# GpSimd in place of VectorE for the argument of the prefix exponent and the low part of block 0's mixed tiles

## The chip, the cores and the metric

One core of a Trainium2 chip runs the whole program. The metric is the device time of one execution in microseconds (us); the kernel before has a median of 1816.48 us over three runs (1815.62 to 1816.57).

## What is computed

The input x has 4 sequences of 1024 positions with 1024 channels; fside has the same shape. First a gated linear recurrence in both directions along the positions (for each channel), then a feed-forward layer with a quantised gelu, then the residual:

```
ek  = exp(min(fside, 30));  ekv = ek * fside
nf, df = forward scans  a = a * decay + ekv,  b = b * decay + ek
nb, db = the same scans backward
num = nf + nb - ekv + exp(min(u + fside, 30)) * fside      (den likewise, without the last factor)
mix = sigmoid(x) * num / max(den, 1e-8) * (0.8 + 0.2 tf)    (decay and tf per sequence, from cond)
h   = mix @ W1.T            (W1: 4096 x 1024)
a   = gelu(round(h / 0.1) * 0.1)
out = x + a @ W2.T          (W2: 1024 x 4096)
```

## The kernel before, in words

A sequence is cut in two halves of 512 positions; a half of a sequence is a block, so there are 8 blocks, and each has 8 tiles (128 channels x 512 positions). Tile g belongs to block g // 8. Even blocks are the late halves (`late` in `tile_of`), odd ones the early halves; blocks run late half first. A late tile needs the state that the early half leaves for it. It is had without a scan: the kernel loads the early half's fside tile as VP, makes the argument EKP = RAMP * ln(decay) + min(VP, 30), takes the exponent on ScalarE with its sum (the prefix of den), and multiplies with VP (L926, the prefix of num). `prefix_argument(g)` makes this argument with two VectorE instructions, L915 (TENSOR_SCALAR) and L918 (SCALAR_TENSOR_TENSOR). EKP is one buffer; VP, V, R, EK, EKV, BON, NUM, DEN have two (index g % 2).

A tile's work on VectorE is split in four parts. Part 0, `weigh`: L926, L929, L931. Part 1, `forward`: scans L959 and L961, and the first step of the reciprocal of the tile before (L937). Part 2, `backward`: scans L978 and L983, with L940 and the output m_st of the tile before (L947) between them, and then `prefix_argument(g + 1)`. Part 3, `sums`: L992 to L1012; its last instruction raises s_gate, on which the loads of V and R of tile g + 2 wait. ScalarE runs the exponents of tile g + 1 (`exps`, which first wait for s_arg of a late tile), then the reciprocal of tile g, then its tanh.

The mixed tile goes to TensorE as a high and a low 16-bit float. For block 0, ScalarE makes the high part (`mix_hi`, L681), and VectorE subtracts it from m_st for the low part (`mix_lo`, L1037), behind part 3 of the next tile. TensorE multiplies each tile of block 0 as it comes (`first_hidden`, L483), then the rest of block 0's hidden layer (L496), and then, block after block, the output product (L562) and the hidden layer of the next block by seven products of halves (L506). While TensorE works on block n, VectorE and ScalarE make the tiles of block n + 1, five of them beside the hidden layer and three beside the output, in an order that is written out by hand in `hidden_block` and behind it.

GpSimd only issues transfers: in a loop over s = 0..7 it waits until R of tile s has landed, and then issues the cast of one eighth of W1 to 16 bits in DRAM (L449), with a cast of W2 at every odd s (L451); then four more casts of W2 (L454) as TensorE's hidden layer proceeds, and 24 copies (L459) during block 0's output. SyncE issues all loads and stores in one hand-written order; in block 0 the first ring loads of weights, which wait for the first two casts, stand ahead of the loads of tiles 2 and 3.

Of the kernel before, what the change touches and what calls it, by code (L numbers as in the profile page):

```python
# [6 lines left out]
ALU = mybir.AluOpType  # L7
# [8 lines left out]
CLIP = 30.0  # L16
# [17 lines left out]
def adaln_ffn_kernel(nc, x, fside, cond, w, u, w1, w2, out):  # L34
    B, HALVES, CT, _, T = x.shape
# [5 lines left out]
    BLOCKS = B * HALVES  # L41
# [11 lines left out]
    with ExitStack() as ctx:  # L53
# [3 lines left out]
        def sem(name):  # L57
            return ctx.enter_context(nc.semaphore(name))
# [21 lines left out]
        mix0 = mo_flat[:, 0:CT * 2 * T].rearrange("p (c a t) -> p c a t", c=CT, a=2)  # L80
# [3 lines left out]
        m_st = sb("m_st", [P, 3, 2, T], F32)  # L84
# [10 lines left out]
        VP = sb("VP", [P, 2, T], F32)  # L95
        EK = sb("EK", [P, 2, T + 1], F32)
        EKV = sb("EKV", [P, 2, T + 1], F32)
        BON = sb("BON", [P, 2, T], F32)
        NUM = sb("NUM", [P, 2, T], F32)
        DEN = sb("DEN", [P, 2, T], F32)  # L100
        EKP = sb("EKP", [P, T], F32)
        RCP = sb("RCP", [P, T], F32)
        RAMP = sb("RAMP", [P, T], F32)
# [22 lines left out]
        lndec = sb("lndec", [P, B, CT], F32)  # L126
# [7 lines left out]
        flag = sb("flag", [1, 1], I32)  # L134
# [11 lines left out]
        s_lndec = sem("s_lndec")  # L146
        s_ramp = sem("s_ramp")
# [7 lines left out]
        s_vp = [sem(f"s_vp{k}") for k in range(2)]  # L155
        s_argr = sem("s_argr")
        s_arg = sem("s_arg")
        s_ekp = sem("s_ekp")
        s_dot = sem("s_dot")
        s_ekx = sem("s_ekx")  # L160
# [17 lines left out]
        s_gate = sem("s_gate")  # L178
# [4 lines left out]
        s_mixhi = sem("s_mixhi")  # L183
        s_mix = sem("s_mix")
# [33 lines left out]
        s_flag = sem("s_flag")  # L218
# [5 lines left out]
        def tile_of(g):  # L224

            n, t = g // CT, g % CT
            return n % BLOCKS // 2, n % 2 == 0, (t % 2) * KH + t // 2, CT * (n // 2) + t
# [9 lines left out]
        def m_slot(g):  # L237
            return (g // 2) % 3
# [205 lines left out]

        @block.gpsimd
        def _(pool):
            for s in range(STEPS):
                pool.wait_ge(s_r[s % 2], 16 * (s // 2 + 1))
                pool.dma_start(w1_half[s], w1_full[s]).then_inc(s_w1cast[s], 16)  # L449
                if s % 2 == 1:  # L450
                    pool.dma_start(w2_half[s // 2], w2_full[s // 2]).then_inc(s_w2cast[s // 2], 16)  # L451
            for d in range(DT // 2, DT):
                pool.wait_ge(s_h0, FPS * (d - 1))
                pool.dma_start(w2_half[d], w2_full[d]).then_inc(s_w2cast[d], 16)  # L454
            for s in range(STEPS):
                pool.wait_ge(s_y, 2 + s)
                pool.wait_ge(s_w1cast[s], 16)
                for r, h, k in ((WP1, 0, 0), (WP2, 0, 1), (WP4, 1, 1)):
                    pool.dma_start(w1s[s][:, r, :, :], w1_quads[s][:, h, :, k, :]).then_inc(s_w1copy[s], 16)  # L459
            for d in range(DT):  # L460
                pool.wait_ge(s_w2cast[d], 16)
            for s in range(STEPS):
                pool.wait_ge(s_w1copy[s], 16 * 3)

        @block.tensor
        def _(pe):
# [409 lines left out]
        def _(dve):  # L876
            v = nc.vector
# [30 lines left out]
                dve.wait_ge(s_lndec, B + 1)  # L908
                dve.wait_ge(s_setup, 6 + B)

            def prefix_argument(g):
                b, late, c, pg = tile_of(g)
                if late:
                    dve.wait_ge(s_ramp, 3)
                    v.tensor_scalar(EKP[:, :], RAMP[:, :], lndec[:, b, c:c + 1], None, ALU.mult).then_inc(s_argr, 1)  # L915
                    dve.wait_ge(s_vp[pg % 2], 16 * (pg // 2 + 1))
                    dve.wait_ge(s_argr, pg + 1)
                    v.scalar_tensor_tensor(out=EKP[:, :], in0=VP[:, pg % 2, :], scalar=CLIP, in1=EKP[:, :],  # L918
                                           op0=ALU.min, op1=ALU.add).then_inc(s_arg, 1)

            def weigh(g):
                b, late, c, pg = tile_of(g)
                k = g % 2
# [91 lines left out]
            def part(p, g):  # L1015

                last = g - 1 if g % CT else None
                if p == 0:
                    weigh(g)
                if p == 1:  # L1020
                    forward(g, last)
                if p == 2:
                    backward(g, last)
                    if g % CT < CT - 1:
                        prefix_argument(g + 1)
                if p == 3:
                    sums(g)

            def divide(g):
                newton(g, 0)  # L1030
                newton(g, 1)
                mixed_out(g)

            def mix_lo(g):
                c = tile_of(g)[2]
                dve.wait_ge(s_mixhi, g + 1)
                v.tensor_tensor(mix0[:, c, 1, :], m_st[:, m_slot(g), g % 2, :], mix0[:, c, 0, :],  # L1037
                                ALU.subtract).then_inc(s_mix, 1)

            def operand_sums(n, q):  # L1040
                g, at = CT * n + 2 * q, KH * (n - 1) + q
# [78 lines left out]
                                       op0=ALU.mult, op1=ALU.not_equal, accum_out=bad[:, at:at + 1]).then_inc(s_chk, 1)  # L1120

            factors()
            prefix_argument(0)
            for t in range(CT):
                for p in range(4):
                    part(p, t)
                    if p == 3 and t > 0:
                        mix_lo(t - 1)
            divide(CT - 1)
            mix_lo(CT - 1)  # L1130

            def hidden_block0(g0):
                for s in range(STEPS):
# [17 lines left out]
            def hidden_block(n, nxt, g0):  # L1151
                for s in range(STEPS):
                    if nxt:
                        if s == 0:
                            prefix_argument(g0)
                        elif s % 2 == 0:
                            part(3, g0 + s // 2 - 1)
                        else:
                            part(1, g0 + s // 2)
                    if s >= 2:  # L1160
                        act_lo(n, s - 2, 1)
                    if s >= 1:
                        quantise22(n, s - 1)
                    if nxt:
                        part(0 if s % 2 == 0 else 2, g0 + s // 2)
                    seed_u4(n, s)
                    if s >= 1:
                        act_lo(n, s - 1, 0)
                if nxt:
                    part(3, g0 + 3)  # L1170
                act_lo(n, LAST - 1, 1)
                if nxt:
                    part(0, g0 + 4)
                quantise22(n, LAST)
                if nxt:
                    part(1, g0 + 4)
                act_lo(n, LAST, 0)
                if nxt:
                    part(2, g0 + 4)
                act_lo(n, LAST, 1)  # L1180
# [71 lines left out]
            def general_block(m):  # L1252
                n = BLOCKS + m
                for t in range(CT):
                    g = CT * n + t
                    prefix_argument(g)
                    weigh(g)
                    forward(g, None)
                    backward(g, None)
                    sums(g)  # L1260
                    newton(g, 0)
                    newton(g, 1)
                    if m > 0:
                        dve.wait_ge(g_h, FT * m)
                    scaled_out(g, ogain_gneg, mix_gen[:, tile_of(g)[2], :])
                for d in range(DT):
                    result(n, d, g_y, DT * m + d + 1, 1.0)
# [46 lines left out]
```

## Time and profile before

| | before |
|---|---|
| median of 3 runs | 1816.48 us |
| the profiled execution's own time | 1813.9 us |
| its span, first to last instruction | 1811.6 us |
| TensorE busy | 1699.9 us, 94% |
| VectorE busy | 1279.5 us, 71% |
| ScalarE busy | 1043.5 us, 58% |
| GpSimd busy | 24.6 us, 1% |

The times of instructions come from the one profiled execution. Start times are counted from the first instruction. A row of the timeline gives start, duration, engine, line, operation and tiles; in square brackets stands how long the engine was idle before it and what ended that. An engine's consecutive instructions overlap a little, so that the distance of two starts, not the duration, is what an instruction costs in a stream. TensorE's busy time is modelled.

### The profile page before, as it was taken

To read this page: it belongs to the slowest core of one execution; us is meant where nothing else is said; L and a number is where in the kernel's file an instruction comes from. 1 tells how busy PE (TensorE), PEld (TensorE's weight loads), DVE (VectorE), ACT (ScalarE), POOL (GpSimd) and SP (SyncE) were. 2 spreads that over 40 slices of the span, in tenths; PEclk is the share of its full clock that TensorE was granted. 3 is DMA by queue.
4 is the path that set the end of the run, shared out by engine and by line. 5 is a ranking of instruction groups with operands and counts; after the bars stand their busy time and mean duration, and the time that the engine had idled before them with its cause. 6 is when DMAs were issued, how large, how long until landed. Compare 5 with 4: busy or idle time off the path is not lost. (4 is left out here: it accounts for less than half of the span.)

```text
span 1811.6 us, 27451 instructions
## 1 busy us (share of the span) xinstructions
PE 1699.9 (94%) x10882; PEld 1067.0 (59%) x10882; DVE 1279.5 (71%) x2008; ACT 1043.5 (58%) x1422; POOL 24.6 (1%) x44
## 2 busy tenths in 40 slices
PE   1459999999999999999999999999999999999998
PEld 0124434687448854588447864488545874478643
DVE  8988885878866786779866777678966687633211
ACT  5458843687437863498526874388634885255300
POOL 0000021000000000000000000000000000000000
PEclk9679999999999999999999999999999999999999
DMA  8747785665546644655446545466445654365442
GB/s 239 178 128 204 253 286 198 204 198 181 162 147 204 195 139 155 198 191 202 162 133 203 187 158 174 144 217 204 156 144 192 195 180 152 120 194 158 145 129 82
DMA packets 109238, 321.16 MB, mean 177 GB/s; under 512 B 12720, under 2 KB 12720, under 8 KB 108592
## 3 DMA queue, kind: packets, MB, share of 16 engines
q1 hardware_dynamic: 106416, 296.28, 50.1%
q0 software_dynamic: 2688, 23.07, 5.5%
q8 instruction: 87, 1.43, 0.3%
q14 instruction: 47, 0.39, 0.1%
HBM read 310.91 MB, written 48.23 MB: 198 GB/s over the span
## 5 line engine op out<-in xcount | busy, mean ns | idle before, releaser
L562 PE MATMUL ps<-act,w_ring 128*128 128x512 f16 x4096 | 890.7, 380 | 4.4 <-DVE y_out L1111 4.4
L506 PE MATMUL ps<-mo,w_ring 128*128 128x256 f16 x6272 | 690.6, 273 | 11.0 <-ACT ps L706 6.1
L562 PEld LDWEIGHTS ps<-act,w_ring 128*128 128x128 f16 x4096 | 401.4, 98 | 485.7 <-issue 8.8
L506 PEld LDWEIGHTS ps<-mo,w_ring 128*128 128x128 f16 x6272 | 612.5, 98 | 90.1 <-issue 7.8
L1102 DVE SCALAR_TENSOR_TENSOR act<-a,act 128x1024 f16<-128x1024 f32 x128 | 156.2, 1221 | 134.7 <-ACT act L755 134.7
L1111 DVE SCALAR_TENSOR_TENSOR y_out<-ps,x_in 128x512 f32<-128x512 f32 x64 | 44.1, 690 | 175.1 <-PE ps L562 107.3
L763 ACT ACTIVATE q<-chk_full 128x1024 int8<-128x1024 f32 x64 | 67.0, 1047 | 144.5 <-DMA chk_full<-in_w_dram 144.5
L749 ACT ACTIVATE a<-q 128x1024 f32<-128x1024 int16 x128 | 135.3, 1057 | 14.6 <-DVE act L1102 10.3
L755 ACT ACTIVATE act<-a 128x1024 f16<-128x1024 f32 x128 | 134.2, 1049 | 0.9
L483 PE MATMUL ps<-mo,w_ring 128*128 128x512 f16 x128 | 42.6, 509 | 89.3 <-DVE mo L1037 89.3
L1119 DVE SCALAR_TENSOR_TENSOR chk_full<-q,chk_full 128x1024 f32<-128x1024 int8 x64 | 78.1, 1220 | 43.8 <-ACT q L763 43.8
L696 ACT ACTIVATE mo<-a 128x1024 f16<-128x1024 f32 x28 | 29.6, 1057 | 128.8 <-DVE a L1048 128.8
L650 ACT ACTIVATE EK<-V 128x512 f32<-128x512 f32 x64 | 39.9, 623 | 109.6 <-DMA V<-in_fside_dram 109.3
L646 ACT ACTIVATE EKP<-EKP 128x512 f32<-128x512 f32 x32 | 20.2, 631 | 133.7 <-DVE EKP L918 133.5
L1085 DVE SCALAR_TENSOR_TENSOR ps<-sp,ps 128x512 f32<-128x512 f32 x56 | 38.8, 692 | 73.7 <-PE ps L506 66.9
L483 PEld LDWEIGHTS ps<-mo,w_ring 128*128 128x128 f16 x128 | 15.4, 125 | 116.0 <-issue 55.8
L496 PE MATMUL ps<-mo,w_ring 128*128 128x512 f16 x384 | 83.0, 379 | 0.0
L670 ACT ACT_TABLE_LOAD x64 | 82.1, 1283 | 1.1
L643 ACT ACT_TABLE_LOAD x64 | 82.1, 1283 | 1.1
L733 ACT ACTIVATE q<-ps 128x512 int16<-128x512 f32 x56 | 33.3, 594 | 85.6 <-PE ps L506 85.6
L978 DVE TENSOR_TENSOR_SCAN EK<-EK,decay 128x512 f32<-128x512 f32 x64 | 81.7, 1277 | 0.1
L983 DVE TENSOR_TENSOR_SCAN EKV<-EKV,decay 128x512 f32<-128x512 f32 x64 | 81.6, 1276 | 0.0
(94 smaller groups left out, 1461.1 us busy)
## 6 DMA issues: line engine op xcount, KB each, us to landing
w_ring<-w1s SPq DMA_DIRECT2D x168, 512.0 KB, 3.7
w_ring<-w_half SPq DMA_DIRECT2D x144, 512.0 KB, 4.2
chk_full<-in_w_dram SPq DMA_DIRECT2D x64, 512.0 KB, 4.6
V<-in_fside_dram SPq DMA_DIRECT2D x64, 256.0 KB, 4.7
R<-in_x_dram SPq DMA_DIRECT2D x64, 256.0 KB, 4.8
w_half<-in_w_dram POOLq DMA_DIRECT2D x16, 1024.0 KB, 7.9
x_in<-in_x_dram SPq DMA_DIRECT2D x64, 256.0 KB, 5.3
out_dram<-y_out SPq DMA_DIRECT2D x64, 256.0 KB, 4.8
```

The lines of the kernel that those rows point to most:

```text
L496: mm = pe.matmul(bank[4 * (s % 2) + j][:, :], w1_ring[:, k, f, c, :], mix0[:, c, p, :], start=(c == 0 and p == 0), stop=(c == CT - 1 and p ...
L506: mm = pe.matmul(dst[:, f, :], wp_ring[:, k, r, f, q, :], mo[:, op, q, p, :], start=(fresh and f == 0 and q == 0 and p == 0), stop=(q == K ...
L562: mm = pe.matmul(y_ps[y][:, :], w2_ring[:, k, f, :], act[:, a, p, :], start=(a == 0 and p == 0), stop=(a == FT - 1 and p == 1))
L643: sc.preload_act_table_set(EXP_SET)
L670: sc.activation(R[:, g % 2, :], R[:, g % 2, :], ACT.Tanh, scale=0.5).then_inc(s_tanh, 1)
L749: sc.activation(a32[:, 2 * h:2 * h + 2, :], q16[:, s % 2, 2 * h:2 * h + 2, :], ACT.Gelu_apprx_tanh, scale=QSTEP).then_inc(s_gelu, 1)
L755: sc.activation(act[:, f:f + 2, 0, :], a32[:, 2 * h:2 * h + 2, :], ACT.Copy, scale=ACT_SCALE).then_inc(s_ahi, 1)
L763: sc.activation(chk_i8, chk_full[:, :], ACT.Copy, scale=W_SCALE).then_inc(s_chki8, 1)
L978: v.tensor_tensor_scan(EK[:, k, 0:T][:, ::-1], EK[:, k, 0:T][:, ::-1], dec(b, c), EK[:, k, T:T + 1], ALU.add, ALU.mult).then_inc(s_dbwd, 1)
L983: v.tensor_tensor_scan(EKV[:, k, 0:T][:, ::-1], EKV[:, k, 0:T][:, ::-1], dec(b, c), EKV[:, k, T:T + 1], ALU.add, ALU.mult).then_inc(s_nbwd, 1)
L1102: v.scalar_tensor_tensor(out=act[:, f:f + 2, 1, :], in0=a32[:, 2 * h:2 * h + 2, :], scalar=ACT_SCALE, in1=act[:, f:f + 2, 0, :], op0=ALU.m ...
L1119: v.scalar_tensor_tensor(out=chk_full[:, :], in0=chk_i8, scalar=1.0 / W_SCALE, in1=chk_full[:, :], op0=ALU.mult, op1=ALU.not_equal, accum_ ...
```

## The change

`prefix_argument` moves from VectorE's program to GpSimd's. There it has three instructions in place of two, since the clip and the sum are made apart: RAMP * ln(decay) into EKP, min(VP, 30) into BON[g % 2] (free until ScalarE writes it for the same tile; the new wait on s_gate guards it), and their sum into EKP. A new semaphore s_kp stands between the last two, and a wait on s_dot guards EKP before it is written again. `mix_lo` moves too, unchanged. In GpSimd's order the argument of tile 0 stands ahead of the first cast; then, for each s, the cast of W1, the argument of tile s + 1, the cast of W2 if there is one, and the low part of tile s - 1. The arguments of blocks 2, 4 and 6 follow behind the last copies. The general path, which only runs when a check on the inputs fails, gets its arguments from GpSimd as well. In `hidden_block` the order of the parts stays.

```diff
--- before.py
+++ after.py
@@ -155,6 +155,7 @@
         s_vp = [sem(f"s_vp{k}") for k in range(2)]
         s_argr = sem("s_argr")
         s_arg = sem("s_arg")
+        s_kp = sem("s_kp")
         s_ekp = sem("s_ekp")
         s_dot = sem("s_dot")
         s_ekx = sem("s_ekx")
@@ -444,11 +445,41 @@
 
         @block.gpsimd
         def _(pool):
+            pl = nc.gpsimd
+
+            def prefix_argument(g):
+                b, late, c, pg = tile_of(g)
+                if late:
+                    pool.wait_ge(s_ramp, 3)
+                    pool.wait_ge(s_lndec, B + 1)
+                    if pg > 0:
+                        pool.wait_ge(s_dot, pg)
+                    pl.tensor_scalar(EKP[:, :], RAMP[:, :], lndec[:, b, c:c + 1], None, ALU.mult).then_inc(s_argr, 1)
+                    pool.wait_ge(s_vp[pg % 2], 16 * (pg // 2 + 1))
+                    pool.wait_ge(s_argr, pg + 1)
+                    if g >= 2:
+                        pool.wait_ge(s_gate, g - 1)
+                    pl.tensor_scalar(BON[:, g % 2, :], VP[:, pg % 2, :], CLIP, None, ALU.min).then_inc(s_kp, 1)
+                    pool.wait_ge(s_kp, pg + 1)
+                    pl.tensor_tensor(EKP[:, :], BON[:, g % 2, :], EKP[:, :], ALU.add).then_inc(s_arg, 1)
+
+            def mix_lo(g):
+                c = tile_of(g)[2]
+                pool.wait_ge(s_mixhi, g + 1)
+                pl.tensor_tensor(mix0[:, c, 1, :], m_st[:, m_slot(g), g % 2, :], mix0[:, c, 0, :],
+                                ALU.subtract).then_inc(s_mix, 1)
+
+            prefix_argument(0)
             for s in range(STEPS):
                 pool.wait_ge(s_r[s % 2], 16 * (s // 2 + 1))
                 pool.dma_start(w1_half[s], w1_full[s]).then_inc(s_w1cast[s], 16)
+                if s + 1 < CT:
+                    prefix_argument(s + 1)
                 if s % 2 == 1:
                     pool.dma_start(w2_half[s // 2], w2_full[s // 2]).then_inc(s_w2cast[s // 2], 16)
+                if s > 0:
+                    mix_lo(s - 1)
+            mix_lo(CT - 1)
             for d in range(DT // 2, DT):
                 pool.wait_ge(s_h0, FPS * (d - 1))
                 pool.dma_start(w2_half[d], w2_full[d]).then_inc(s_w2cast[d], 16)
@@ -457,10 +488,18 @@
                 pool.wait_ge(s_w1cast[s], 16)
                 for r, h, k in ((WP1, 0, 0), (WP2, 0, 1), (WP4, 1, 1)):
                     pool.dma_start(w1s[s][:, r, :, :], w1_quads[s][:, h, :, k, :]).then_inc(s_w1copy[s], 16)
+            for g in range(2 * CT, CT * BLOCKS):
+                prefix_argument(g)
             for d in range(DT):
                 pool.wait_ge(s_w2cast[d], 16)
             for s in range(STEPS):
                 pool.wait_ge(s_w1copy[s], 16 * 3)
+
+            pool.wait_ge(s_flag, 1)
+            needs_general = pool.value_load(flag[0:1, 0:1], min_val=0, max_val=1)
+            with pool.If(needs_general > 0):
+                for g in range(CT * BLOCKS, 2 * CT * BLOCKS):
+                    prefix_argument(g)
 
         @block.tensor
         def _(pe):
@@ -907,16 +946,6 @@
                 v.tensor_scalar(lndec[:, :, :], lndec[:, :, :], LN_DECAY_MIN, None, ALU.max).then_inc(s_lndec, 1)
                 dve.wait_ge(s_lndec, B + 1)
                 dve.wait_ge(s_setup, 6 + B)
-
-            def prefix_argument(g):
-                b, late, c, pg = tile_of(g)
-                if late:
-                    dve.wait_ge(s_ramp, 3)
-                    v.tensor_scalar(EKP[:, :], RAMP[:, :], lndec[:, b, c:c + 1], None, ALU.mult).then_inc(s_argr, 1)
-                    dve.wait_ge(s_vp[pg % 2], 16 * (pg // 2 + 1))
-                    dve.wait_ge(s_argr, pg + 1)
-                    v.scalar_tensor_tensor(out=EKP[:, :], in0=VP[:, pg % 2, :], scalar=CLIP, in1=EKP[:, :],
-                                           op0=ALU.min, op1=ALU.add).then_inc(s_arg, 1)
 
             def weigh(g):
                 b, late, c, pg = tile_of(g)
@@ -1021,8 +1050,6 @@
                     forward(g, last)
                 if p == 2:
                     backward(g, last)
-                    if g % CT < CT - 1:
-                        prefix_argument(g + 1)
                 if p == 3:
                     sums(g)
 
@@ -1030,12 +1057,6 @@
                 newton(g, 0)
                 newton(g, 1)
                 mixed_out(g)
-
-            def mix_lo(g):
-                c = tile_of(g)[2]
-                dve.wait_ge(s_mixhi, g + 1)
-                v.tensor_tensor(mix0[:, c, 1, :], m_st[:, m_slot(g), g % 2, :], mix0[:, c, 0, :],
-                                ALU.subtract).then_inc(s_mix, 1)
 
             def operand_sums(n, q):
                 g, at = CT * n + 2 * q, KH * (n - 1) + q
@@ -1120,14 +1141,10 @@
                                        op0=ALU.mult, op1=ALU.not_equal, accum_out=bad[:, at:at + 1]).then_inc(s_chk, 1)
 
             factors()
-            prefix_argument(0)
             for t in range(CT):
                 for p in range(4):
                     part(p, t)
-                    if p == 3 and t > 0:
-                        mix_lo(t - 1)
             divide(CT - 1)
-            mix_lo(CT - 1)
 
             def hidden_block0(g0):
                 for s in range(STEPS):
@@ -1151,12 +1168,10 @@
             def hidden_block(n, nxt, g0):
                 for s in range(STEPS):
                     if nxt:
-                        if s == 0:
-                            prefix_argument(g0)
-                        elif s % 2 == 0:
+                        if s % 2 == 1:
+                            part(1, g0 + s // 2)
+                        elif s > 0:
                             part(3, g0 + s // 2 - 1)
-                        else:
-                            part(1, g0 + s // 2)
                     if s >= 2:
                         act_lo(n, s - 2, 1)
                     if s >= 1:
@@ -1253,7 +1268,6 @@
                 n = BLOCKS + m
                 for t in range(CT):
                     g = CT * n + t
-                    prefix_argument(g)
                     weigh(g)
                     forward(g, None)
                     backward(g, None)
```

## Rows read from the trace of the kernel before

**Rows 1.** The page: busy time and share of each engine; the slices.
```profile
PE 1699.9 (94%) x10882; PEld 1067.0 (59%) x10882; DVE 1279.5 (71%) x2008; ACT 1043.5 (58%) x1422; POOL 24.6 (1%) x44
...
PE   1459999999999999999999999999999999999998
...
DVE  8988885878866786779866777678966687633211
ACT  5458843687437863498526874388634885255300
```

**Rows 2.** Timeline of PE: the start of its unbroken work, and its later gaps.
```profile
123.34 8.59 PE L483 MATMUL ps<-mo,w_ring 128*128 128x512 f16 x32 [8.33 <-DVE mo L1037]
131.76 83.04 PE L496 MATMUL ps<-mo,w_ring 128*128 128x512 f16 x384
...
546.10 3.28 PE L506 MATMUL ps<-mo,w_ring 128*128 128x256 f16 x26 [0.86 <-DVE mo L1054]
550.53 9.66 PE L506 MATMUL ps<-mo,w_ring 128*128 128x256 f16 x87 [1.15 <-ACT ps L706]
...
759.34 5.84 PE L506 MATMUL ps<-mo,w_ring 128*128 128x256 f16 x52 [0.32 <-ACT ps L706]
```

**Rows 3.** Timeline of DVE in block 0: the first argument, one tile's period, the last tile.
```profile
8.85 0.49 DVE L915 TENSOR_SCALAR EKP<-RAMP,lndec 128x512 f32<-128x512 f32 x1
...
60.52 0.48 DVE L915 TENSOR_SCALAR EKP<-RAMP,lndec 128x512 f32<-128x512 f32 x1
...
61.72 0.69 DVE L992 TENSOR_TENSOR DEN<-DEN,EK 128x512 f32<-128x512 f32 x1
...
65.91 0.68 DVE L1037 TENSOR_TENSOR mo<-m_st,mo 128x512 f16<-128x512 f32 x1
66.51 0.68 DVE L926 SCALAR_TENSOR_TENSOR EKV<-EKP,VP 128x512 f32<-128x512 f32 x1
...
74.99 0.48 DVE L915 TENSOR_SCALAR EKP<-RAMP,lndec 128x512 f32<-128x512 f32 x1
...
123.87 0.69 DVE L937 TENSOR_TENSOR DEN<-DEN,RCP 128x512 f32<-128x512 f32 x1 [0.59 <-ACT RCP L666]
```

**Rows 4.** Groups by line and shape, whole span: busy us, mean ns of one.
```profile
L992 DVE TENSOR_TENSOR DEN<-DEN,EK 128x512 f32<-128x512 f32 x64 | 43.8, 684 | 0.0
L959 DVE TENSOR_TENSOR_SCAN NUM<-decay,pre_n,EKV 128x512 f32<-128x512 f32 x32 | 41.0, 1280 | 0.8
L929 DVE TENSOR_SCALAR EK<-EK 128x512 f32<-128x512 f32 x64 | 27.0, 422 | 2.0 <-ACT EK L650 1.8
...
L650 ACT ACTIVATE EK<-V 128x512 f32<-128x512 f32 x64 | 39.9, 623 | 109.6 <-DMA V<-in_fside_dram 109.3
```

**Rows 5.** The page's DMA issues: count, KB each, median us to landing.
```profile
R<-in_x_dram SPq DMA_DIRECT2D x64, 256.0 KB, 4.8
w_half<-in_w_dram POOLq DMA_DIRECT2D x16, 1024.0 KB, 7.9
```

**Rows 6.** Timeline of ACT at the start: the first exponent of an argument.
```profile
10.18 0.63 ACT L646 ACTIVATE EKP<-EKP 128x512 f32<-128x512 f32 x1 [0.94 <-DVE EKP L918]
```

**Rows 7.** Timelines of POOL and DVE: a cast's issue and the scan beside it.
```profile
30.08 0.49 POOL L449 DMA_DIRECT2D w_half<-in_w_dram  x1 [19.44 <-DMA R<-in_x_dram]
...
29.75 1.28 DVE L983 TENSOR_TENSOR_SCAN EKV<-EKV,decay 128x512 f32<-128x512 f32 x1
```

**Rows 8.** Timelines of DVE and ACT at the output of block 1.
```profile
507.31 0.69 DVE L918 SCALAR_TENSOR_TENSOR EKP<-VP,EKP 128x512 f32<-128x512 f32 x1 [7.43 <-DMA VP<-in_fside_dram]
...
508.03 0.63 ACT L646 ACTIVATE EKP<-EKP 128x512 f32<-128x512 f32 x1 [17.58 <-DVE EKP L918]
...
511.38 0.63 ACT L664 ACTIVATE RCP<-DEN 128x512 f32<-128x512 f32 x1 [0.87 <-DVE DEN L1003]
```

**Rows 9.** Stretches of 4 us: busy (count) of each engine, PE clock, DMA.
```profile
120.00:124.00 4.00, 0.66 (x2) 0.29 (x3) 3.38 (x9) 3.00 (x4) 0.00 (x0) 0.50 0.09 16
...
128.00:132.00 4.00, 4.00 (x21) 1.78 (x19) 0.00 (x0) 3.03 (x4) 0.00 (x0) 1.00 0.00 0
```

## The prediction

> **What bounds the kernel now.** I read the busy shares and the slices first. TensorE is busy 94% of the span, but its row of slices begins 1, 4, 5 and is full from the fourth slice on, while VectorE is full over those first slices [rows 1]. So there are two stretches with different limits. TensorE's own row of time gives the border: from 131.76 us it works almost without a gap to the end, and what it loses is little: about 2 us (0.86 and 1.15) where it enters a block with late tiles in preparation, against 0.32 us where the tiles in preparation are early ones [rows 2]. Behind the border VectorE's share is spare time; ahead of it the time is whatever makes the last mixed tile. Everything that moves that border moves the end one for one.
>
> Ahead of the border VectorE is back to back: a late tile takes 14.47 us (60.52 to 74.99, the start of the same instruction in two tiles), with no idle time in it; its first wait of the stretch worth naming is 0.59 us for ScalarE's reciprocal of the last tile [rows 3]. ScalarE waits for VectorE there, and TensorE sits idle 8.33 us before its last two tiles [rows 2]. VectorE sets the border.
>
> **The change, part by part.** (1) Two instructions per late tile leave VectorE: L915 and L918 hold it from 60.52 to 61.72, so 1.20 us. Seven of these lie in block 0's back-to-back stretch (tiles 1 to 7): 8.4 us. (2) mix_lo leaves it: 65.91 to 66.51, 0.60 us. Six of the eight are in the stream (tiles 0 to 5), 3.6 us; that of tile 6 lies in the 0.59 us wait for the reciprocal and is worth nothing, and that of tile 7 is the last step of the path [rows 3]. Together 12.0 us off VectorE's stream, 12.7 us a tile in place of 14.47. What comes next on that path is then ScalarE and the transfers. ScalarE's slices there are about half full, some 7 us in a tile [rows 1], and it would get the argument early in the tile. A load of R lands 4.8 us after its issue [rows 5], and is issued a whole tile ahead of its use. Both fit in 12.7 us. The casts go out behind the argument and the mixed tile of the step before, so later within a tile, and the first behind the first argument. The ring loads that wait for the first two casts stand in SyncE's queue ahead of the loads of tiles 2 and 3; those wait for VectorE's gate, the end of the sums of tiles 0 and 1, anyhow, and a cast lands 7.9 us after its issue [rows 5], so I cost this at nothing. The cover fails if that landing grows to well over 12 us.
>
> (3) GpSimd gets four instructions for these tiles in place of three: ramp times a scalar, min, add, and the subtraction. No row shows GpSimd at 128x512. Bounds: not less than VectorE's own 0.48 and 0.68, since nothing suggests that it is the faster engine; not more than the slowest 128x512 row, the scan with 1.28 [rows 3, 4]. I take 0.62 for the two with one tensor input, ScalarE's row for 128x512, and 1.25 for the two with two inputs, near the scan: together 3.74 us a tile (bounds 2.3 and 5.1). The Trainium skill (GPSIMD Engine Reference, section Elementwise — side-by-side cycle accounting) gives 4497 ns for a two-input add of 2048 elements; an estimate from it is about 1.2 us for 512, and the sum by it would be the same within 1 us.
>
> (4) At both ends GpSimd's length is bare. The first argument takes VectorE from 8.85 to ScalarE's start at 10.18, 1.33 us [rows 3, 6]; on GpSimd 0.62 + 0.62 + 1.25 and some 0.24 us of handing over, 2.73: +1.4 us (bounds +0.3 and +2.8). The last mix_lo: 1.25 for 0.69, +0.6 us (0 to +0.6).
>
> (5) Whether GpSimd's time is beside VectorE's or in its place decides the sign. What the rows show: a two-input instruction of 512 elements takes 0.684 us on VectorE, a one-input one 0.422 [rows 4]. So VectorE reads two operands' worth at once, and one-input work uses that for double speed: it has two ways into the memory and nearly each of its instructions in this stretch keeps both in use. GpSimd reads the same partitions. The only case of both together is a cast's issue at 30.08 under a scan that keeps its usual 1.28 us [rows 7], which writes a few descriptors and reads no tensor, so it excludes nothing. My forecast takes it that one of the two stands still while the other reads. The page SBUF — State Buffer of the Trainium skill, section Who interferes with whom, speaks against this change in the same sense: a VectorE instruction with two SBUF inputs and a GpSimd instruction that reads SBUF exclude each other for a whole instruction. No row here can confirm it.
>
> Then each GpSimd instruction takes its length from VectorE's stream, less the 0.09 us by which VectorE's instructions overlap anyhow (0.69 long, 0.60 apart) [rows 3]. Arguments: 7 x (2.49 - 0.27 - 1.20) = +7.1 us. Mixed tiles: 7 x (1.25 - 0.09) - 3.6 = +4.5 us (seven now, since tile 6's falls beside the sums). With both ends, +13.6 us at the border.
>
> (6) Beyond the border, 24 more arguments leave VectorE, 28.8 us, all under TensorE. At the entry to a late-fed block the path runs through one of them: VP of the last tile arrives at 507.31, VectorE adds, ScalarE starts at 508.03 and has 0.87 us to spare before its next wait ends [rows 8]. On GpSimd min and add take 1.87 us where 0.69 stood, so ScalarE starts about 1.2 us later, of which 0.87 us is covered: +0.3 us at each of three such entries, +1 us (bounds 0 and +4.5, if each instruction must also wait for one of VectorE's). That VectorE no longer stands 7.43 us for VP gives nothing, as its next result waits for that same ScalarE chain.
>
> Sum: 13.6 + 1 = +14.6 us on the profiled execution's 1813.9 us (span 1811.6), 1828.5. The median of the runs stands 2.6 us above that execution, so 1831 us. By bounds: with GpSimd at VectorE's durations 7 x (1.65 - 0.27 - 1.20) + 7 x 0.59 - 3.6 + 0.3 = +2.1 us, 1819; with 1.28 for each instruction 7 x (3.84 - 0.27 - 1.20) + 7 x 1.19 - 3.6 + 3.4 + 4.5 = +29 us, 1846. I hold durations near the middle likelier than either end.
>
> **Rivals.** *Side by side (faster).* If the two engines read without disturbing each other, the terms are -12.0 + 1.4 + 0.6 + 1 = -9.0 us: 1807.5 us (1804 to 1811). For it: 12.0 us of plain VectorE work on the path that sets the border, a GpSimd that is 1% busy [rows 1], and the cast that disturbed no scan. Against: the two ways into memory that VectorE's rows show in use. It decides from the point at which a GpSimd instruction costs VectorE less than four tenths of its length (12.0 - 2.0 us left to lose, against 7 x 3.74 = 26 us of GpSimd time). TensorE's last tile could add up to 3 us in it, if the earlier tile 6 leaves a pause in which the clock falls: it stands at 0.50 before that burst and at 1.00 after 128 us [rows 9]; I expect the pause too short.
>
> *Partly in each other's way.* Scans take about twice a plain instruction's time for as many elements (1.28 against 0.684) [rows 4], and may leave half the reads free; the argument falls mostly beside scans. Then some 3 us of the 12.0 are left or lost after the ends: 1813 to 1820, centre 1817.
>
> *The work is moved but arrives late.* GpSimd's queue now has, ahead of an argument, the wait for R, a cast (0.49 us) and the mixed tile of two tiles before, which waits for ScalarE's copy. An argument may start 0.7 us into a tile (behind L926) and its exponent is needed at the tile's end: 12.7 - 0.7 - 2.5 - 0.7, some 8 us, are spare. Were GpSimd held out by VectorE's stream until VectorE itself has to wait for the argument, a tile would cost 12.7 + 2.5 + 0.7 (the exponent) and more: about 17 us, +20 us in all, 1838. This is within the slower side.
>
> **How the numbers follow.** Forecast (one stands still for the other) 0.47; held out until VectorE waits 0.08; partly 0.15; side by side 0.30. "The same" is within 0.2%, 3.6 us, about what a measurement of this kernel can tell from no change: most of "partly" and the lowest part of the forecast, 0.16; slower 0.54; faster 0.30. The forecast's own range is 1819 to 1843. The range that should hold 8 in 10 must reach into the faster case: 1805 to 1840.
>
> **What would show it.** In the changed kernel's profile: the distance between the starts of L926 in two of block 0's tiles, 12.7 us if side by side, about 16 by my forecast; VectorE's two-input instructions longer than 0.69 us, or idle time between them, where a GpSimd instruction runs; GpSimd's own mean at L915's and L918's successors, 0.62 and 1.25; TensorE's border at 145 us, or at 122; the first exponent at 11.6; and TensorE's gaps at entries to late-fed blocks of 2 us still. I am wrong if VectorE's instructions keep their 0.68 us beside GpSimd's.

## The result, and the profile after

The changed kernel takes 1832.73 us (median of 4 runs, 1831.88 to 1834.77) where the kernel before took 1816.05 us on the same chip: a ratio of 1.0095, 95% interval 1.0077 to 1.0112, so 0.95% slower. The forecast was 1831 us, its own range 1819 to 1843.

First the page of the changed kernel, its busy shares and GpSimd's slices, then GpSimd's groups by shape (busy us, mean ns of one, idle time before and what ended it). The lines of the file have shifted: GpSimd's L457, L462 and L464 are the product, the clip and the sum, L469 is the low part; VectorE's L955 was L926, and TensorE's L522, L535, L545 and L601 were L483, L496, L506 and L562.

```profile
PE 1706.5 (93%) x10882; PEld 1067.3 (58%) x10882; DVE 1289.6 (70%) x1936; ACT 1045.7 (57%) x1422; POOL 201.2 (11%) x148
...
POOL 4530021121110000111120000012120000000000
```
```profile
L462 POOL TENSOR_SCALAR BON<-VP 128x512 f32<-128x512 f32 x32 | 65.3, 2039 | 664.4 <-DMA VP<-in_fside_dram 663.0 <-POOL EKP L457 0.3
L457 POOL TENSOR_SCALAR EKP<-RAMP,lndec 128x512 f32<-128x512 f32 x32 | 50.5, 1578 | 314.0 <-DVE EKV L955 306.2 <-DVE lndec L946 7.8
L464 POOL TENSOR_TENSOR EKP<-BON,EKP 128x512 f32<-128x512 f32 x32 | 43.0, 1344 | 2.7
L469 POOL TENSOR_TENSOR mo<-m_st,mo 128x512 f16<-128x512 f32 x8 | 17.3, 2168 | 44.3 <-ACT mo L720 44.3
```

VectorE has 72 instructions fewer (64 of the arguments, 8 low parts) and is yet busy some 10 us longer than before [rows 1]: some of those that stayed became longer.

TensorE's timeline, the start of its unbroken work and later gaps:

```profile
130.56 9.98 PE L522 MATMUL ps<-mo,w_ring 128*128 128x512 f16 x32 [7.05 <-POOL mo L469]
140.37 83.04 PE L535 MATMUL ps<-mo,w_ring 128*128 128x512 f16 x384
...
558.20 3.28 PE L545 MATMUL ps<-mo,w_ring 128*128 128x256 f16 x26 [1.98 <-DVE mo L1075]
562.56 89.24 PE L545 MATMUL ps<-mo,w_ring 128*128 128x256 f16 x816 [1.09 <-ACT ps L745]
...
1258.38 24.61 PE L545 MATMUL ps<-mo,w_ring 128*128 128x256 f16 x224 [0.43 <-DVE q L1116]
```

The border is at 140.37 where it was at 131.76 [rows 2]: 8.6 us of the 18.5 us by which the span grew. At the entry to block 2 the same matmuls stand at 562.56 against 550.53, 12.0 us later; at the end it is 18.2 us. So about half of the loss lies behind the border.

Here is why VectorE's stream became longer. One tile of block 0, VectorE first, then GpSimd, in the changed kernel:

```profile
41.42 0.69 DVE L955 SCALAR_TENSOR_TENSOR EKV<-EKP,VP 128x512 f32<-128x512 f32 x1
...
42.49 1.06 DVE L960 TENSOR_TENSOR EKV<-EK,V 128x512 f32<-128x512 f32 x1
43.66 1.28 DVE L988 TENSOR_TENSOR_SCAN NUM<-decay,pre_n,EKV 128x512 f32<-128x512 f32 x1
44.86 1.56 DVE L990 TENSOR_TENSOR_SCAN DEN<-decay,pre_d,EK 128x512 f32<-128x512 f32 x1
46.36 1.75 DVE L966 TENSOR_TENSOR DEN<-DEN,RCP 128x512 f32<-128x512 f32 x1
...
54.52 1.51 DVE L1038 TENSOR_TENSOR NUM<-NUM,V 128x512 f32<-128x512 f32 x1
...
56.68 0.69 DVE L955 SCALAR_TENSOR_TENSOR EKV<-EKP,VP 128x512 f32<-128x512 f32 x1
```
```profile
42.33 1.57 POOL L457 TENSOR_SCALAR EKP<-RAMP,lndec 128x512 f32<-128x512 f32 x1 [1.61 <-DVE EKV L955]
44.04 2.18 POOL L462 TENSOR_SCALAR BON<-VP 128x512 f32<-128x512 f32 x1
46.31 1.26 POOL L464 TENSOR_TENSOR EKP<-BON,EKP 128x512 f32<-128x512 f32 x1
53.09 2.40 POOL L469 TENSOR_TENSOR mo<-m_st,mo 128x512 f16<-128x512 f32 x1 [5.52 <-ACT mo L720]
```

The instructions that became L960, L990, L966 and L1038, in the kernel before:

```profile
53.11 0.69 DVE L931 TENSOR_TENSOR EKV<-EK,V 128x512 f32<-128x512 f32 x1
...
55.11 1.26 DVE L961 TENSOR_TENSOR_SCAN DEN<-decay,pre_d,EK 128x512 f32<-128x512 f32 x1
56.30 0.69 DVE L937 TENSOR_TENSOR DEN<-DEN,RCP 128x512 f32<-128x512 f32 x1
...
64.58 0.68 DVE L1009 TENSOR_TENSOR NUM<-NUM,V 128x512 f32<-128x512 f32 x1
```

Four of VectorE's instructions are longer than their usual selves, each beside one of GpSimd's four: L960 by 0.37 us (1.06 for 0.69), L990 by 0.30, L966 by 1.06, L1038 by 0.83. Together 2.56 us. The tile takes 56.68 - 41.42 = 15.26 us, and 14.47 - 1.20 - 0.60 + 2.56 is 15.23. Nothing else changed in it. GpSimd waits too: L462 takes 2.18 us where it starts under a scan that already runs and 1.49 at the kernel's start, where VectorE is idle; L469 takes 2.40 us under the row of two-input sums and 1.15 at the end of block 0, where VectorE is idle.

### The profile page after: what moved, and what is told of

Read it like the earlier page. It is cut to its first block and busy times, and to the rows that moved or that the text cites. A ratio compares the mean times of both kernels' runs of the same rounds, so it can differ in the third digit from the quotient of the medians.

```text
span 1830.1 us, 27520 instructions
## 1 busy us (share of the span) xinstructions
PE 1706.5 (93%) x10882; PEld 1067.3 (58%) x10882; DVE 1289.6 (70%) x1936; ACT 1045.7 (57%) x1422; POOL 201.2 (11%) x148
## 5 line engine op out<-in xcount | busy, mean ns | idle before, releaser
L601 PE MATMUL ps<-act,w_ring 128*128 128x512 f16 x4096 | 889.5, 379 | 4.9 <-DVE y_out L1132 4.9
L545 PE MATMUL ps<-mo,w_ring 128*128 128x256 f16 x6272 | 694.0, 273 | 17.5 <-DVE mo L1075 9.0
L601 PEld LDWEIGHTS ps<-act,w_ring 128*128 128x128 f16 x4096 | 401.1, 98 | 485.2 <-issue 7.6
L545 PEld LDWEIGHTS ps<-mo,w_ring 128*128 128x128 f16 x6272 | 612.2, 98 | 100.8 <-issue 13.4
L1123 DVE SCALAR_TENSOR_TENSOR act<-a,act 128x1024 f16<-128x1024 f32 x128 | 156.9, 1226 | 136.2 <-ACT act L794 136.2
L462 POOL TENSOR_SCALAR BON<-VP 128x512 f32<-128x512 f32 x32 | 65.3, 2039 | 664.4 <-DMA VP<-in_fside_dram 663.0
L522 PE MATMUL ps<-mo,w_ring 128*128 128x512 f16 x128 | 46.5, 546 | 94.0 <-POOL mo L469 94.0
L522 PEld LDWEIGHTS ps<-mo,w_ring 128*128 128x128 f16 x128 | 16.4, 133 | 123.7 <-issue 63.8
L457 POOL TENSOR_SCALAR EKP<-RAMP,lndec 128x512 f32<-128x512 f32 x32 | 50.5, 1578 | 314.0 <-DVE EKV L955 306.2
L535 PE MATMUL ps<-mo,w_ring 128*128 128x512 f16 x384 | 83.0, 379 | 0.0
```

The costliest lines, as they stand in the source:

```text
L462: pl.tensor_scalar(BON[:, g % 2, :], VP[:, pg % 2, :], CLIP, None, ALU.min).then_inc(s_kp, 1)
L522: mm = pe.matmul(bank[4 * s + j][:, :], w1_ring[:, slots[2 * s + j // 2], j % 2, c, :], mix0[:, c, p, :], start=(t == 0 and p == 0), stop= ...
L535: mm = pe.matmul(bank[4 * (s % 2) + j][:, :], w1_ring[:, k, f, c, :], mix0[:, c, p, :], start=(c == 0 and p == 0), stop=(c == CT - 1 and p ...
L545: mm = pe.matmul(dst[:, f, :], wp_ring[:, k, r, f, q, :], mo[:, op, q, p, :], start=(fresh and f == 0 and q == 0 and p == 0), stop=(q == K ...
L601: mm = pe.matmul(y_ps[y][:, :], w2_ring[:, k, f, :], act[:, a, p, :], start=(a == 0 and p == 0), stop=(a == FT - 1 and p == 1))
L1123: v.scalar_tensor_tensor(out=act[:, f:f + 2, 1, :], in0=a32[:, 2 * h:2 * h + 2, :], scalar=ACT_SCALE, in1=act[:, f:f + 2, 0, :], op0=ALU.m ...
```

## The experiments

Each is compared with the kernel before on its own chip (ratio, 95% interval); borders are TensorE's first L496 in the profiled execution, 131.76 us before. A difference in us behind a ratio is that ratio times the time of the kernel before. The diffs show only the lines that matter. In the profiled executions of these runs ln(decay) is ready 0.2 to 0.8 us sooner than in the one of the kernel before (8.01 to 8.65 us in place of 8.82), a difference that no edit before it explains, and it lies in the borders. What block 0's stream itself gained or lost is therefore read from the first to the last of its eight L926, 98.99 us before. Where nothing else is said, the whole computation is done.

**One part alone: the low parts.**

```diff
-                    if p == 3 and t > 0:
-                        mix_lo(t - 1)        # VectorE, block 0
+                if s > 0:
+                    mix_lo(s - 1)            # GpSimd, behind the casts of step s
...
             def mixed_out(g):
+                if 6 <= g < CT + 6:
+                    dve.wait_ge(s_mix, g - 5)
```

The last wait is not in the changed kernel; it keeps a mixed tile from being overwritten before its low part is made.

> Only the eight low parts of block 0's mixed tiles are on GpSimd; all arguments stay on VectorE. Theory (the two engines exclude each other while they read): in the changed kernel each low part lengthened VectorE's L1038 from 0.68 to 1.51 us, so 7 x 0.83 = +5.8 us, less 6 x 0.60 = 3.6 us that leave VectorE, and +0.5 us for the bare last one: +2.7 us on before, and L1038's successor at 1.5 us in block 0. Rival (side by side): -3.6 + 0.5 = -3.1 us, with VectorE's instructions at 0.68 us.

Measured: 1814.18 us, ratio 0.9995 (0.9985 to 1.0004), which is -0.9 us; border 132.17, +0.4 us. Neither number came out (+2.7 and -3.1 us were expected); the lengthened instructions did. GpSimd's queue had no arguments in it, so the low parts ran at other places than in the changed kernel, four of the six in the stream beside L1025 and two beside a scan (L972):

```profile
35.86 1.53 DVE L1025 SCALAR_TENSOR_TENSOR NUM<-R,NUM 128x512 f32<-128x512 f32 x1
...
67.73 1.99 DVE L972 TENSOR_TENSOR_SCAN NUM<-decay,pre_n,EKV 128x512 f32<-128x512 f32 x1
...
67.01 1.62 POOL L452 TENSOR_TENSOR mo<-m_st,mo 128x512 f16<-128x512 f32 x1 [14.51 <-ACT mo L692]
```

The scan takes 1.99 us in place of 1.28, +0.71 us, and L1025 1.53 in place of 0.69, +0.84 us, where 0.60 leave. The stream is 100.12 us long, 1.1 us more than before, and 4 x 0.84 + 2 x 0.71 - 3.6 = +1.2. So a low part moved was worth nothing at either of the two places where it fell.

**One part alone: block 0's arguments.**

```diff
-            prefix_argument(0)               # VectorE
-                    if g % CT < CT - 1:
+                    if g % CT < CT - 1 and g >= CT:
                         prefix_argument(g + 1)
+            prefix_argument(0)               # GpSimd, three instructions
+                if s + 1 < CT:
+                    prefix_argument(s + 1)
```

> Only block 0's arguments are on GpSimd; later arguments and all low parts stay on VectorE. Theory: a tile's three GpSimd instructions cost VectorE 0.37 + 0.30 + 1.06 = 1.73 us (L960, L990, L966 of the changed kernel) where 1.20 us leave, 7 x 0.53 = +3.7 us, and the first argument comes 3.2 us later (4.5 us of GpSimd for 1.3): +6.9 us on before, TensorE's unbroken stretch at about 138.7. Rival (side by side): -8.4 + 3.2 = -5.2 us.

Measured: 1821.38 us, ratio 1.0034 (1.0021 to 1.0047), which is +6.2 us; border 139.22, +7.5 us.

```profile
139.22 83.04 PE L518 MATMUL ps<-mo,w_ring 128*128 128x512 f16 x384
```

The theory had +6.9 us: the time is 0.7 us below it and the border 0.6 above. The stream is 102.68 us long, +3.7 us as computed, and the first L926 starts at 13.98 in place of 10.93. This part carries 7.5 of the 8.6 us by which the border moved in the changed kernel.

**One part alone: the arguments of blocks 2, 4 and 6.** GpSimd's loop stands behind the copies, and VectorE keeps only tiles 0 to 7.

```diff
+            for g in range(2 * CT, CT * BLOCKS):
+                prefix_argument(g)           # GpSimd, three instructions
...
-                    if g % CT < CT - 1:
+                    if g < CT - 1:
                         prefix_argument(g + 1)
...
-                            prefix_argument(g0)
+                            pass
```

> Only the arguments of blocks 2, 4 and 6 are on GpSimd; block 0 is as before. In the changed kernel TensorE lost 9.7 us more behind its border than before, some 2 us of it at each of three block entries. Theory (a longer chain from VP to the exponent, 3.4 us of GpSimd for 0.7): all of that stays, +9 us, with the border at 131.8 unmoved. Rival (those losses follow from the disturbed block 0, or from the low parts): under +1 us.

Measured: 1824.59 us, ratio 1.0051 (1.0035 to 1.0068), +9.3 us; border 131.63, unmoved. The loss behind the border (9.6 us in the changed kernel) comes from these 24 arguments, with block 0 undisturbed. Its size is less certain than that: TensorE's way from the border to its last work is 1674.35 us in the profiled execution of the kernel before and 0.8 to 2.8 us longer in those of six runs here that change nothing behind the border, so some 1 to 3 us of the 9.6, and of the 12.2 in this run's own profile, may be that one execution. The three parts by themselves add up to -0.9 + 6.2 + 9.3 = +14.6 us where the whole cost 17.2; with some 2 to 3 us of uncertainty on each, the difference is not more than noise.

**Half of each argument: only the product on GpSimd.**

```diff
+                    pl.tensor_scalar(EKP[:, :], RAMP[:, :], lndec[:, b, c:c + 1], None, ALU.mult).then_inc(s_argr, 1)   # GpSimd
-                    v.tensor_scalar(EKP[:, :], RAMP[:, :], lndec[:, b, c:c + 1], None, ALU.mult).then_inc(s_argr, 1)    # VectorE
```

> GpSimd makes only the product RAMP * ln(decay) of every argument, with one tensor input; the clip and sum stay on VectorE as one instruction, and so do the low parts. Theory of exclusion with the price by instruction: VectorE loses 0.37 us a tile and is rid of 0.60, 7 x -0.23 = -1.6 us, and +1.1 us at the start: -0.5 us in block 0. Behind the border, theory of the long chain: nothing lost, since the product is made before VP arrives: in all -0.5 us, the same as before. Rival (later losses come from disturbing VectorE): several us slower still.

Measured: 1814.78 us, ratio 0.9997 (0.9988 to 1.0007); border 131.41. The forecast of -0.5 us came out in both. In block 0 the price by instruction holds: the stream is 97.42 us long, 1.6 us less than before (0.37 paid for 0.60, seven times), and the first L926 starts 1.1 us later. Behind the border nothing is lost beyond what the unchanged runs show, although GpSimd makes 24 products there beside VectorE's work: what hurts there is what comes behind VP's landing, the clip and the sum.

**The disturbance by itself.** Three runs keep all the work of before and add 16 GpSimd instructions of 128x512 in block 0, two behind each L926. Their results are used by nobody.

```diff
+                for j in range(2):
+                    pl.tensor_tensor(a32[:, 2 + j, :], RAMP[:, :], RAMP[:, :], ALU.add)        # first run
+                    pl.memset(a32[:, 2 + j, :], 1.0)                                           # second
+                    pl.tensor_scalar(a32[:, 2 + j, :], RAMP[:, :], 2.0, None, ALU.mult)        # third
```

The diff leaves out the waits: each of the 16 starts when the one before it has ended, and ScalarE waits for the last of them before its work on block 0's hidden layer.

> The kernel before, unchanged in all its work, with 16 added GpSimd instructions of two 128x512 float32 inputs in block 0, two behind each L926, whose results nobody uses. It measures the disturbance by itself. Theory: VectorE stands still while GpSimd reads, about 1.0 us each: +16 us, TensorE's unbroken stretch at about 148, VectorE's two-input instructions of 1.6 to 2.1 us in weigh, forward and backward. Rival (side by side; the changed kernel lost by order and by GpSimd's lateness): within 0.5 us of before.

> As the run with 16 added two-input instructions, but they are 16 fills (MEMSET) of the same size, which write and read nothing. Theory (it is the reading that excludes): within 1 us of before. Rival (any GpSimd access to the memory holds VectorE): about +0.5 us each, +8 us.

(A fill writes its tile and reads none; that is what the sentence above means.)

> As the run with 16 added two-input instructions, but with one input each (TENSOR_SCALAR). Theory: 0.3 to 0.4 us each, as L960 and L990 showed in the changed kernel, though each lasts 1.5 us: +5 to +6 us. Rival (VectorE is held for the whole length of a GpSimd instruction): 16 x 1.5 = +24 us.

Measured: two inputs 1825.09 us, ratio 1.0059 (1.0043 to 1.0074), border 141.48, +9.7 us; fills 1815.96 us, ratio 1.0004 (0.9994 to 1.0013), border 131.73; one input 1818.85 us, ratio 1.0026 (1.0016 to 1.0035), border 135.93, +4.2 us. The timelines of VectorE and GpSimd with two inputs:

```profile
56.25 1.41 DVE L944 TENSOR_TENSOR EKV<-EK,V 128x512 f32<-128x512 f32 x1
57.76 1.87 DVE L972 TENSOR_TENSOR_SCAN NUM<-decay,pre_n,EKV 128x512 f32<-128x512 f32 x1
...
56.01 1.09 POOL L456 TENSOR_TENSOR a<-RAMP 128x512 f32<-128x512 f32 x1 [12.26 <-issue]
57.19 1.37 POOL L456 TENSOR_TENSOR a<-RAMP 128x512 f32<-128x512 f32 x1
```

with one input:

```profile
69.22 0.98 DVE L944 TENSOR_TENSOR EKV<-EK,V 128x512 f32<-128x512 f32 x1
...
71.50 1.56 DVE L974 TENSOR_TENSOR_SCAN DEN<-decay,pre_d,EK 128x512 f32<-128x512 f32 x1
...
69.01 1.52 POOL L456 TENSOR_SCALAR a<-RAMP 128x512 f32<-128x512 f32 x1 [10.15 <-issue]
70.61 2.25 POOL L456 TENSOR_SCALAR a<-RAMP 128x512 f32<-128x512 f32 x1
```

and with fills:

```profile
66.78 0.69 DVE L944 TENSOR_TENSOR EKV<-EK,V 128x512 f32<-128x512 f32 x1
67.58 1.28 DVE L972 TENSOR_TENSOR_SCAN NUM<-decay,pre_n,EKV 128x512 f32<-128x512 f32 x1
...
66.52 1.27 POOL L456 MEMSET a<- 128x512 f32 x2 [7.22 <-issue]
```

So side by side falls: two-input instructions of 1.09 and 1.37 us took 0.72 and 0.59 us from VectorE, one-input instructions of 1.52 and 2.25 us only 0.29 and 0.30, and two fills of 0.6 us nothing. The rows even give the moment of release. VectorE's L944 should have ended at 56.94 and ended at 57.66, so it got going at 56.97, 0.96 us after GpSimd's start and 0.1 us before GpSimd's end; in the changed kernel L966 got going 0.15 us before L464 ended. Two inputs thus held VectorE for very nearly the whole instruction. With one input it is otherwise: L944 got going 0.5 us after the start of an instruction that lasts 1.52, and L974, like L960 and L990 in the changed kernel, 1.0 to 1.1 us before the end of GpSimd's. That VectorE waits just for the part in which GpSimd reads fits all of these rows, and the fills, but no row shows GpSimd's reading by itself. This is the step where the rule of the Trainium skill (SBUF — State Buffer, section Who interferes with whom) and the runs meet: reading against two inputs excludes, writing does not, as it says; that the pair is held "for the whole instruction" the rows with two inputs come close to and those with one do not bear out. I had expected 1.0 us each for the first run. The stream is 108.12 us long there, +9.1 us for 14 of the 16, so 0.65 us each: GpSimd's instruction starts 0.24 us ahead of L944 and 0.57 us ahead of L972, and that much of the hold costs VectorE nothing, where in the changed kernel L464 starts 0.05 us ahead of L966 and costs 1.06. One input cost 0.3 us each in the same count, at the low end of what I had expected.

**A late signal without any reading.** In blocks 2, 4 and 6, VectorE makes the arguments as before, but ScalarE also waits for 12 small fills that GpSimd makes behind VP's landing.

```diff
+                    for j in range(12):
+                        if fills > 0:
+                            pool.wait_ge(s_kp, fills)
+                        nc.gpsimd.memset(unused[:, :], 1.0).then_inc(s_kp, 1)
+                        fills += 1
                     act_e.wait_ge(s_arg, pg + 1)
+                    act_e.wait_ge(s_kp, 12 * (pg - CT + 1))
```

> The kernel before, with every argument made by VectorE as ever, but in blocks 2, 4 and 6 ScalarE's exponent also waits for 12 small fills (MEMSET 128x128) that GpSimd makes one after the other once VP has landed. GpSimd reads nothing, so VectorE is not disturbed; only the exponent is late, by some 2 to 4 us behind VP's landing as in the run with only the late blocks' arguments on GpSimd. Theory (those lose 9 us by a longer chain from VP to the exponent): +6 to +12 us, with TensorE's idle time of 3 us in place of 2 at the entries to blocks 2, 4 and 6 and small gaps in the hidden layers of blocks 1, 3 and 5. Rival (they lose it because GpSimd's reading holds VectorE): within 1 us of before.

Measured: 1820.74 us, ratio 1.0033 (1.0021 to 1.0045), +6.0 us. ScalarE's exponent at the output of block 1, and TensorE's entry to block 2:

```profile
510.39 0.63 ACT L661 ACTIVATE EKP<-EKP 128x512 f32<-128x512 f32 x1 [18.75 <-POOL unused L471]
...
547.84 93.76 PE L519 MATMUL ps<-mo,w_ring 128*128 128x256 f16 x842 [1.98 <-DVE mo L1069]
```

The exponent is 2.4 us later than before (508.03 [rows 8]), and TensorE enters block 2 at 547.84 for 546.10 [rows 2]. Lateness alone gives 6.0 of the 9.3 us, about two thirds, though the intervals of the two runs overlap; it falls at the entries (1.7 to 2.2 us each). The small gaps in hidden layers, which I had expected here too, did not come: none waits for VectorE's L1095 (L1116 in the changed kernel). They are the work of the exclusion, and the changed kernel's rows show how, VectorE first, then GpSimd, then TensorE in the hidden layer of block 1:

```profile
429.49 1.51 DVE L1123 SCALAR_TENSOR_TENSOR act<-a,act 128x1024 f16<-128x1024 f32 x1 [3.71 <-ACT act L794]
430.91 2.31 DVE L988 TENSOR_TENSOR_SCAN NUM<-decay,pre_n,EKV 128x512 f32<-128x512 f32 x1
...
436.08 0.68 DVE L1116 SCALAR_TENSOR_TENSOR q<-ps,sp 128x512 int16<-128x512 f32 x1
...
429.30 1.49 POOL L462 TENSOR_SCALAR BON<-VP 128x512 f32<-128x512 f32 x1 [3.80 <-DMA VP<-in_fside_dram]
430.88 1.27 POOL L464 TENSOR_TENSOR EKP<-BON,EKP 128x512 f32<-128x512 f32 x1
...
436.90 1.36 PE L545 MATMUL ps<-mo,w_ring 128*128 128x256 f16 x11 [0.29 <-DVE q L1116]
```

L1123 takes 0.29 us longer than the 1.22 of its row before (L1102), beside the clip, and the scan 1.03 us longer, beside the sum; L1116 comes that much later, and TensorE waits for it. A run with such reading alone in these blocks was not made, so the third is the difference of two runs, and its cause is read from these rows.

**ScalarE in place of GpSimd.** The product of block 0's tiles is made by ScalarE, ahead of its exponent.

```diff
+                if g < CT:
+                    act_e.wait_ge(s_dot, pg)     # tile 0: s_ramp and s_lndec
+                    sc.activation(EKP[:, :], RAMP[:, :], ACT.Copy, scale=lndec[:, b, c:c + 1]).then_inc(s_argr, 1)
```

> Before, with the product RAMP * ln(decay) of block 0's tiles made by ScalarE (an activation Copy with ln(decay) as scale) in front of the exponents; all else as before. ScalarE is half idle there and its reads disturb no one by any row so far. Theory: 7 x 0.60 = -4.2 us, 1812 us, each VectorE instruction unchanged; a late tile takes 13.9 us. Rival (ScalarE gets to it too late, so that VectorE waits for it before L918): same as before or slower.

Measured: 1811.40 us, ratio 0.9980 (0.9971 to 0.9989), border 127.69, 4.1 us earlier.

```profile
58.67 0.69 DVE L925 SCALAR_TENSOR_TENSOR EKP<-VP,EKP 128x512 f32<-128x512 f32 x1
...
72.55 0.68 DVE L925 SCALAR_TENSOR_TENSOR EKP<-VP,EKP 128x512 f32<-128x512 f32 x1
...
66.81 0.72 ACT L650 ACTIVATE EKP<-RAMP,lndec 128x512 f32<-128x512 f32 x1
```

A tile takes 72.55 - 58.67 = 13.88 us, 0.59 less than 14.47, and no instruction of VectorE in it is longer. The same idea as the change, for one of the two instructions and in block 0 alone, on an engine whose reading costs VectorE nothing in these rows, is the only version here whose interval lies below the kernel before.

## Why the prediction was right, and where it was not

The sign and the place were right: VectorE's stream in block 0 sets the border, and GpSimd's work went into it, not beside it. A tile takes 15.26 us, where 12.7 would have meant side by side and about 16 was forecast. The total, 1831 against 1832.7 us, is right partly by luck, since two terms were too large and two too small:

| term | predicted | measured in the profiled execution |
|---|---|---|
| first argument | +1.4 us | +3.4 us from ln(decay) to the exponent; +2.8 us at the first L955, as ln(decay) came 0.75 us sooner |
| arguments and low parts in the stream | +7.1 + 4.5 = +11.6 us | +5.5 us (first to last L955, and the last tile) |
| last low part | +0.6 us | +0.5 us (1.15 for 0.69) |
| the border | +13.6 us | +8.6 us |
| behind the border | +1 us, 0 to +4.5 | +9.6 us |
| in all | +14.6 us | +18.2 us at TensorE's last work |

The medians lie 16.7 us apart. The first argument and the loss behind the border came out above my bounds for them (+2.8 and +4.5 us).

*GpSimd's durations* (step 3). I gave the one-input instructions the shorter time, 0.62 us, and the two-input ones the longer, 1.25. The second was right (1.26), the first was not even inside my bounds: 1.49 and 1.57 us, longer than the sum of two tensors. The start shows it bare, GpSimd and then ScalarE in the changed kernel:

```profile
8.25 1.57 POOL L457 TENSOR_SCALAR EKP<-RAMP,lndec 128x512 f32<-128x512 f32 x1 [7.82 <-DVE lndec L946]
9.98 1.49 POOL L462 TENSOR_SCALAR BON<-VP 128x512 f32<-128x512 f32 x1 [0.16 <-POOL EKP L457]
11.55 1.26 POOL L464 TENSOR_TENSOR EKP<-BON,EKP 128x512 f32<-128x512 f32 x1
...
12.85 0.63 ACT L685 ACTIVATE EKP<-EKP 128x512 f32<-128x512 f32 x1 [4.37 <-POOL EKP L464]
```

*What an instruction takes from VectorE* (step 5). I took its whole length less 0.09 us. A one-input instruction holds VectorE only for its first half microsecond, and any instruction costs only that part of its hold that lies under a two-input instruction of VectorE. A tile's argument cost 1.73 us where I had 2.22, a low part 0.83 where I had 1.16. More than twice the length that I gave the one-input instructions therefore did not hurt the stream. With these prices the stream's term is 7 x (1.73 - 1.20) + 7 x 0.83 - 3.6 = +5.9 us, and +5.5 was measured.

*Behind the border* (step 6). The place and the mechanism were right, the size was not. GpSimd and ScalarE at the output of block 1 in the changed kernel:

```profile
490.59 4.47 POOL L462 TENSOR_SCALAR BON<-VP 128x512 f32<-128x512 f32 x1 [15.81 <-DMA VP<-in_fside_dram]
...
517.40 2.02 POOL L462 TENSOR_SCALAR BON<-VP 128x512 f32<-128x512 f32 x1 [14.99 <-DMA VP<-in_fside_dram]
519.51 1.26 POOL L464 TENSOR_TENSOR EKP<-BON,EKP 128x512 f32<-128x512 f32 x1
...
520.81 0.63 ACT L685 ACTIVATE EKP<-EKP 128x512 f32<-128x512 f32 x1 [16.17 <-POOL EKP L464]
```

From VP to the exponent 3.4 us where 0.7 stood: 2.7 us more, less the 0.87 us of cover that I had named, gives 1.8 us, and the entry to block 2 moved by 2.05. I had 0.3 because of the 0.62 us above. The run with late fills shows this part by itself. The entries to blocks 4 and 6 moved by 2.0 and 1.2 us. What I had not seen at all are the hidden layers of blocks 1, 3 and 5 (about 1.3 us each), where I counted VectorE's 28.8 us of relief as neither gain nor loss, and did not count what GpSimd's reading takes from VectorE there, as I had in block 0. The row at 490.59 shows the other side of the exclusion, GpSimd held out for 3 us by VectorE; it is the rival "arrives late" in small, and TensorE had no gap in the 60 us behind it.

*The rivals.* Side by side is refuted by the run with two-input instructions: +9.7 us at the border for work that nobody uses. "Partly in each other's way" had the better picture of the mechanism, though for the wrong reason: scans were lengthened like all others (1.99 for 1.28), and what is free is the time in which GpSimd's instruction no longer holds VectorE, or holds it where it needs nothing. Work that arrives late decided nothing in block 0, as reckoned. TensorE's clock in its last tile changed nothing: in both kernels it is granted 0.50 until about the end of the last low part, and from there to the border it is 4.15 us, 4.30 before.

## What to carry to other kernels

Before work is moved from VectorE to GpSimd, count how many of VectorE's instructions around it have two inputs in SBUF: beside those, a GpSimd instruction that reads cost VectorE 0.3 to 0.4 us here for one input of 512 elements and 0.6 to 1.1 us for two. So moving a two-input instruction of 0.60 us gained nothing in these runs, and moving a one-input one of 0.60 us gained 0.2 us a tile, most of which its late result at the start ate up. What GpSimd's reading costs beside a stream of one-input VectorE instructions, no run here shows. Look then at who waits for the result: GpSimd needed 4.5 us where two VectorE instructions needed 1.3, and most of that difference was bare where an input arrived late. ScalarE, half idle beside the same stream, took one of the two instructions at no cost to VectorE.

## What the runs showed of the hardware that I had not expected

- A GpSimd TENSOR_SCALAR of 128x512 float32 takes 1.49 us (min) and 1.57 us (product with a column), a TENSOR_TENSOR add 1.1 to 1.3 us and a fill 0.6 us: one input is slower than two.
- The slower one holds VectorE less: a two-input instruction of VectorE got going about 0.5 us after the start of a one-input GpSimd instruction, 1.0 us before its end, and about 1.0 us after the start of a two-input one, 0.1 us before its end.
- Two-input instructions in a row on VectorE hold GpSimd out beyond one of them: a clip took 4.47 us for 1.49 beside such a row. By its usual length it got going at 493.57, under L1032 (493.30 to 493.72), the first in that row with one tensor input.
